# The first of a round's two C products issued ahead of the background products of the round before, and evictions of projections moved one round back

## The reference

```
q, k, v = split_heads(x @ W + b) for each of Wq, Wk, Wv      # (b, 16, 4096, 16)
scores   = q k^T / 4
sparsity = max(scores) - mean(scores)          # per query, over 4096 keys
top_idx  = the 307 queries of largest sparsity, per batch and head
out      = zeros; out[top_idx] = softmax(q[top_idx] k^T / 4) v
x = layernorm(x + out @ Wo + bo)
# then a mixing block with two gates:
xr, xk = mu * x + (1 - mu) * (x shifted by one token)
x = layernorm(x + sigmoid(xr @ W_r) * (relu(xk @ W_k)^2 @ W_v))
```

## Time and profile before

| what | value |
|---|---|
| time of 3 runs, median (lowest to highest) | 3449.08 us (3445.66 to 3450.98) |
| the profiled execution's own time | 3456.68 us |
| its span in the profile | 3454.9 us |
| PE, DVE, ACT, POOL busy over the span | 90%, 85%, 83%, 43% |
| granted clock of TensorE, mean over the span | 0.97 |

### The profile page before, as it was taken

How to read it: one execution, slowest core, us unless ns; L and a number is a source line. 1 busy time by engine, 2 the same in 40 slices (tenths; PEclk the granted TensorE clock), 3 DMA queues, 4 the chain that set the end, 5 groups by cost and what they waited for, 6 DMA issues and landing times.

```text
span 3454.9 us, 58997 instructions
## 1 busy us (share of the span) xinstructions
PE 3099.2 (90%) x15985; PEld 1433.1 (41%) x15985; DVE 2950.1 (85%) x5969; ACT 2873.2 (83%) x6445; POOL 1482.1 (43%) x2619
## 2 busy tenths in 40 slices
PE   6999999998899998998999888899988898897678
PEld 3334333343344433433444344444444443344466
DVE  4989988899979888888899888888988898886578
ACT  5889888889779999899899877699977699894555
POOL 2210022100136643553456356665555653447744
PEclk8999999999999999999999999999999999997899
DMA  6333222216021251141021251211142131013122
GB/s 178 80 100 113 64 75 82 82 30 18 15 44 32 39 33 31 33 33 32 19 36 31 46 48 42 49 37 35 31 41 48 35 33 32 14 20 15 19 79 69
DMA packets 262608, 163.63 MB, mean 47 GB/s; under 512 B 167877, under 2 KB 241797, under 8 KB 258181
## 3 DMA queue, kind: packets, MB, share of 16 engines
q1 hardware_dynamic: 254181, 156.41, 25.0%
q0 software_dynamic: 6144, 1.37, 0.5%
q10 hardware_dynamic: 1952, 2.10, 0.2%
HBM read 111.86 MB, written 47.86 MB: 46 GB/s over the span
## 4 chain that ended last, share of the span: by engine, by line
ACT 29%; PE 27%; issue 20%; DVE 19%; POOL 2%; DMA 1%; ACTq 0%; DVEq 0%; SPq 0%; POOLq 0%
ACT AB L941 21%; DVE JK L1100 11%; PE CP L669 8%; PE DP L673 7%; ACT E L979 5%; ACT msk L962 2%; PE PV L780 1%; PE PV L781 1%; PE BP L765 1%; PE BP L615 1%; DVE VF L1311 1%; DVE fst L1270 1%; DVE SPr L1100 1%; PE PV L803 1%; PE PV L615 1%
## 5 line engine op out<-in xcount | busy, mean ns | idle before, releaser
L1100 DVE CUSTOM_DVE_ANT_0 JK<-DP,AB 128x1024 bf16<-128x1024 f32 x2048 | 2468.0, 1222 | 366.5 <-DVE SPr L1100 129.9
L941 ACT ACTIVATE AB<-CP 128x512 f32<-128x512 f32 x4096 | 2226.6, 598 | 282.7 <-PE CP L669 234.2
L669 PE MATMUL CP<-KS,QS 128*128 128x512 f16 x4096 | 1424.0, 388 | 94.7 <-ACT AB L941 20.1
L673 PE MATMUL DP<-KS,QS 128*128 128x512 f16 x4096 | 1236.9, 384 | 61.1 <-DVE SPr L1100 54.6
L1506 POOL TENSOR_TENSOR SCR<-E 128x307 f16<-128x307 f32 x953 | 661.8, 707 | 585.1 <-ACT E L979 578.3
L669 PEld LDWEIGHTS CP<-KS,QS 128*128 128x128 f16 x4096 | 392.3, 96 | 887.5 <-ACT AB L941 752.7
L673 PEld LDWEIGHTS DP<-KS,QS 128*128 128x128 f16 x4096 | 360.9, 98 | 386.0 <-DVE SPr L1100 171.0
L979 ACT ACTIVATE E<-BP 128x307 f32<-128x307 f32 x871 | 379.6, 436 | 30.3 <-PE BP L765 29.2
L1355 POOL TENSOR_SCALAR SCR<-SCR 128x48 f16<-128x48 f16 (+2 forms) x122 | 49.2, 403 | 540.6 <-DVE SCR L1066 316.4
L765 PE MATMUL BP<-QT,KA 128*128 128x307 f16 x871 | 258.3, 297 | 20.4 <-ACT QT L971 18.4
L780 PE MATMUL PV<-E,XT 128*128 128x307 bf16 x512 | 161.0, 315 | 26.6 <-POOL SCR L1506 25.9
(11 more groups left out here) (369 smaller groups left out, 2997.3 us busy)
## 6 DMA issues: line engine op xcount, KB each, us to landing
KS<-KTC SPq DMA_DIRECT2D x256, 128.0 KB
QS<-QSC SPq DMA_DIRECT2D x512, 64.0 KB
KA<-KTC SPq DMA_DIRECT2D x128, 128.0 KB
QN<-SCR SPq DMA_DIRECT2D x16, 544.0 KB, 3.5
SCR<-in_L_attn_x SPq DMA_DIRECT2D x16, 512.0 KB, 6.3
AO<-E SPq DMA_DIRECT2D x16, 512.0 KB, 7.1
VF<-in_L_attn_x SPq DMA_DIRECT2D x64, 128.0 KB, 2.2
VF<-AO SPq DMA_DIRECT2D x64, 128.0 KB, 2.2
```

What stands on the lines that cost most here:

```text
L669: pe.matmul(o, qs, ks[j][:, 1, :], start=True, stop=True).then_inc(sc_c, 1)
L673: r = pe.matmul(o[:, 512 * j:512 * j + 512], qs, ks[j][:, 0, :], start=True, stop=True)
L941: act.activation(AB[p % 3][:, 512 * j:512 * j + 512], BANK["C%d" % j], ACT.Abs).then_inc(ab_full, 1)
L1100: dve.tensor_tensor_reduce(out=JK[p % 2][:], in0=BANK["D%d" % u], in1=AB[p % 3][:], scale=1.0, scalar=-3.0e38, op0=ALU.add, op1=ALU.max, a ...
```

## The change

Two things are moved and nothing is added or removed.

First, the C0 product of round p + 1 becomes a token of its own, `lead`. Where the background or attention step of round p holds one of `pv`, `xt`, `kmm`, `qmm`, `qtr`, `val`, this token is put right ahead of the first such token. So for an attention step PE now runs C1, D, D, score product, C0 of the next round, value product, value product; and in a projection round C1, D, D, C0 of the next round, then the two products. 1231 of the 2047 rounds get such a lead. In the others C0 is issued at the start of its round as before.

Second, the evictions are tokens of their own (`xtev`, `kev`, `qev`, `qtev`, `vev`). While rounds run, they stand one step later, behind the part of `main` of the next round on ACT and DVE; only the key projections that DVE evicts (`hi` = 0) and everything in the start (`fast`) keep their place. A bank whose eviction is late is not given to the next product (`state["late"]`).

```diff
-            if b != state["open"]:
+            if b not in (state["open"], state["late"]):
                 return b
...
             for hi in (1, 0):
                 bk = state["open"] = bank()
+                evict = [("kev", b, half, c, hi, bk, fast)]
                 for part in range(3):
-                    yield [("kmm", b, half, c, hi, part, bk, fast)]
+                    step = waiting + [("kmm", b, half, c, hi, part, bk, fast)]
+                    waiting = []
+                    if part == 2:
+                        state["open"], state["late"] = None, bk if hi and not fast else None
+                    yield step + (evict if part == 2 and (fast or not hi) else [])
+                    if part == 2 and hi and not fast:
+                        waiting, state["late"] = evict, None
...
+    def with_lead(step, p):
+
+        for i, token in enumerate(step):
+            if token[0] in ("pv", "xt", "kmm", "qmm", "qtr", "val") and p + 1 < NB * H * NP:
+                return step[:i] + [("lead", p + 1)] + step[i:]
+        return step
...
-            plan.extend(step or [])
+            plan.extend(with_lead(step or [], n * NP + p))
...
+            def lead_(p):
+                n = p // NP
+                led.add(p)
                 if p % NP == 0:
-                    pe.wait_ge(l_k[i], 128 * (n // 2 + 1))
+                    pe.wait_ge(l_k[n % 2], 128 * (n // 2 + 1))
                 if p % 32 == 0:
                     pe.wait_ge(l_h[p // 32 % 2], 128 * (n + 1))
...
+                qs, ks = scores(p)
+                o = claim("C0")
+                pe.matmul(o, qs, ks[0][:, 1, :], start=True, stop=True).then_inc(sc_c, 1)
+                owed["C0"] = ((ab_full, 2 * p + 1),)
+
+            def main(p):
+                u = p % 2
+                if p not in led:
+                    lead_(p)
+                qs, ks = scores(p)
+                o = claim("C1")
+                pe.matmul(o, qs, ks[1][:, 1, :], start=True, stop=True).then_inc(sc_c, 1)
+                owed["C1"] = ((ab_full, 2 * p + 2),)
```

More of the change, by code:

```diff
@@ L113, in product @@
         def product(c):
+            waiting = []
             for j in range(2):
                 bk = state["open"] = bank()
+                evict = [("qev", b, half, c, j, bk, fast)]
                 for part in range(3):
-                    yield [("qmm", b, half, c, j, part, bk, fast)]
-                state["open"] = None
+                    step = waiting + [("qmm", b, half, c, j, part, bk, fast)]
+                    waiting = []
+                    if part == 2:
+                        state["open"], state["late"] = None, None if fast else bk
+                    yield step + (evict if part == 2 and fast else [])
+                state["late"] = None
+                waiting = [] if fast else evict
+            if not fast:
+                yield waiting + [("split", k0 + c, "q", b, half, c, fast)]
         def store(c):
+            waiting = []
             for j in range(2):
-                yield [("qtr", b, half, c, j, bank(), fast)]
-            yield [("qstore", b, half, c)]
+                bk = bank()
+                evict = [("qtev", b, half, c, j, bk)]
+                state["late"] = None if fast else bk
+                yield waiting + [("qtr", b, half, c, j, bk, fast)] + (evict if fast else [])
+                waiting, state["late"] = [] if fast else evict, None
+            yield waiting + [("qstore", b, half, c)]
         if fast:
@@ L145, in values @@
                     bk = state["open"] = bank()
-                yield [("val", b, t, part, bk)] + ([("azero", t // 16, t // 2 % 8)] if b == 0 and t % 2 + part == 0 else [])
-            state["open"] = None
+                step = waiting + [("val", b, t, part, bk)]
+                waiting = []
+                if part == 2:
+                    state["open"], state["late"] = None, bk
+                yield step + ([("azero", t // 16, t // 2 % 8)] if b == 0 and t % 2 + part == 0 else [])
+            waiting, state["late"] = [("vev", b, t, bk)], None
+        yield waiting
     def select(g):
@@ L879, in xt, with kev @@
                                accum_out=xpart[:, k, c:c + 1]).then_inc(xt_act, 1)
-            def kmm(b, half, c, hi, part, bank, fast):
-                if part == 2 and hi:
+            def kev(b, half, c, hi, bank, fast):
+                if hi:
                     m = (2 * b + half) * 4 + c
@@ L1057, in kbar, with kev @@
                 dve.tensor_tensor(cols[:, SH], cols[:, BK], cols[:, KB], ALU.subtract).then_inc(kb_dve, 1)
-            def kmm(b, half, c, hi, part, bank, fast):
-                if part == 2 and not hi:
+            def kev(b, half, c, hi, bank, fast):
+                if not hi:
                     m = (2 * b + half) * 4 + c
```

62 lines of the change are left out of this document (30 added, 32 removed).

## The result

The changed kernel takes 3397.91 us (median of 4 runs, 3396.41 to 3403.29) against 3447.76 us for the kernel before (4 runs). The ratio is 0.9857, with a 95% interval of 0.9845 to 0.9869. That is 50 us less, 1.4%; I had forecast 3390.

The account below looks back on a forecast made before the run. No engine saturates throughout; a PE-ACT wait loop, closed by PE's order, was taken to set attention and projection rounds. Gains of 23 + 1 + 3 + 4 + 12 + 9 + 4 + 3 = 59 us from 3449 gave 3390, range 3350 to 3430.

Parts of the forecast that it names:

- Attention, 23 us: 622 plain attention rounds fall from 1.337 us to ACT's floor of 1.300, gaining 0.037 each, 23 us.
- The loop: Attention: PE and ACT wait for each other, 2.66 us per two rounds; C0 ahead of value products makes it 2.39.
- The moved wait: Attention: PE stands 0.05 to 0.08 us at C0, replacing the old wait at C1, so it costs nothing.
- The sign that I had given: Attention stretch: rounds of 1.30, ACT without gaps, a short wait of C0's load and nearly none for C1.
- the bubble stays: Rival, chance 0.12: the wait only moves from C1 to C0, attention gains nothing, projections half; 3426 us.
- slower: Rival, chance 0.08: C0's exposed weight load and semaphore add to PE's attention rounds, 1.40 us each; 3484 us.
- More: Rival, chance 0.17: evictions are hidden and ACT goes a bit under 1.30 in attention; 94 us gained, 3355 us.
- It does nothing: Rival, chance 0.05: ACT's and DVE's total work bounds the kernel at the same length; 3449 us.
- First rounds of a head, value products alone: 16 first rounds gain about 0.16 us each, 3 us; 30 value-product rounds go from 1.27 to 1.144, 4 us.
- Query chunks with their transposes, 9 + 4 us: Six product rounds 8.42 us against 9.03, 14 chunks, 9 us; transposes 4.2 against 4.47, 14 times, 4 us.
- Key chunks, 12 us: Key projections: six rounds take 8.14 us against 9.17, with eviction stalls of 0.28 and 0.12; 12 chunks, 12 us.
- Value projections, 3 us: Value projection rounds go from 1.275 us to 1.257, set by DVE's floor; 192 rounds, 3 us.

Follow-up runs that it names:

- second profile: The kernel before, unedited, profiled once more: 3449.28 us, where the execution profiled first took 3456.68.
- the swap: Changed kernel with the two halves of a key chunk in the other order, the half DVE evicts first: 3393.16 us, ratio 0.9853 to the kernel before.
- the experiment on the bank: Changed kernel, but a value projection isn't given the bank whose eviction stands in its own step: 3389.55 us, ratio 0.9838 to the kernel before.

## Why the prediction was right

The time lies in the range and the gain is 50 us where I had 59. The mechanism of the largest term, attention, is shown. That the total came so near is in part luck: all terms of the forecast lie in the 2048 rounds, and there the change gains 43 us, not 59. The start and the tail, on which the forecast had put nothing, gave another 8 between the two first profiles. By the steps:

- **Attention, 23 us.** Summed over the 622 rounds the changed kernel takes 811.6 us; the kernel before took 838.0, and 836.7 in its second profile. That is 25 us. The loop, PE's order as its cause and ACT as the next bound are each shown: by the product left out in the kernel before (1.297), by the same in the changed one (no change), and by the shorter exponential (1.261). A round of the stretch is 1.296, not 1.300; the mean of all 622 is 1.305, from 1.347. The 45 rounds with one-hot work, for which I had 1 us, lose 1.5 instead (75.2 to 76.7); no experiment looks into that.
- **The moved wait.** I had put 0.05 to 0.08 us of standing on PE at C0; its products show 0.02. The sign that I had given, a short wait of the load for C0 and nearly none for C1, came out only in part: the loads wait 0.26 and 0.16, and the one for C1 still stands 0.05 us behind the end of ACT's pair (it was 0.04). Both fit in a round that ACT sets. So the rivals "the bubble stays" and "slower" are refuted, with attention rounds at 1.296. "More" is refuted too: attention stopped at ACT's bound, and the evictions were not hidden. "It does nothing" is refuted by the time.
- **First rounds of a head, value products alone.** 3 and 4 us forecast; 2.7 (16 rounds, 41.6 to 38.9 us) and 3.7 (30 rounds, 38.1 to 34.4).
- **Query chunks with their transposes, 9 + 4 us.** Measured 0.85 a chunk, 12 us for 14. The six product rounds take 8.02, which is 7.74 and the one stall of 0.28; the second eviction lands in the round behind them. The stalls of 0.28 and 0.40 for an eviction on ACT were 0.26 (rounds of 1.55 against 1.29) and 0.41 (1.55 against 1.144).
- **Key chunks, 12 us.** Mis-sized. Six rounds take 8.54, not 8.14, and the chunk gains 0.63, 7 us for 12. The stall for DVE's eviction was taken as 0.12 and is 0.52: the third round takes 1.81. The prediction gives no working for its 0.12. Behind this eviction come rounds in which DVE itself is the bound, so none of its time is won back there. Placed first, in front of rounds that PE bounds, it costs 0.22, which the swap shows.
- **Value projections, 3 us.** Where they run by themselves the gain is there: 96 rounds from 122.37 to 120.33. Beside the search the change costs 10 us, which the prediction missed. It had taken 3 us for all 192 rounds from DVE's floor and had put no term on which bank the next projection draws. The bank drawn too early accounts for these 10, as the rounds with a value projection show (57.1 to 47.1 us in the experiment on the bank). The stretch also holds 29 rounds with a value projection where it held 27: the late evictions add one round behind the first batch's value projections and one behind the transposes of the input, so later background work stands two rounds later.
- **The start and the tail** were 4 us each shorter in the changed kernel's profile than in that of before. The start was between 60.2 and 67.0 us long in the traces of this study, whatever the edit, so I put nothing on it. The tail took 336.3 and 335.9 us in the two profiles of the kernel before and 331.6 to 334.5 in the kernels that move C0 or the evictions and leave all products in; why is open.

Against the second profile of the kernel before, the rounds sum up to 3044.7 - 3001.3 = 43 us: 25 (attention) + 7 (key) + 12 (query) + 3 (first rounds of a head) + 4 (value products alone) + 2 (value projections by themselves) = 53 gained, 10 given back in the search stretch.

That the two moves help in projections only together was nowhere in the prediction. I had costed the lead and the late eviction as one.

## What to carry to other kernels

When two engines hand single buffers to and fro, walk the loop over two turns and sum it from starts in the timeline. What one engine does between two products that the other waits for is in the loop even if that engine is not the bound, and moving it out of the loop pays until some engine's own work is the bound. A product that is issued earlier needs the consumer's queue in the same order: an early C0 whose reader stands behind an eviction that waits for a later product made query chunks longer than no change at all (18.25 against 16.95 us). And when the release of a buffer is moved later, look at who else draws from that pool, in the stretch where most draw from it. A cost that is read from one kind of stretch, here value projections without the search, need not hold where two kinds of work meet.

## What the runs showed of the hardware

ACT's instructions read as longer when ACT is the bound. In the changed kernel the absolute value's mean is 621 ns against 598 for the same 4096 instructions, and the exponential's 476 against 436, though the rounds are shorter. By stretch it is plainer. The rows are the absolute value in the attention stretch of the kernel before, in its five rounds without value products (where ACT was the bound already), in the attention stretch of the changed kernel, and there with the shorter exponential, where PE is the bound:

```profile
L941 ACT ACTIVATE AB<-CP 128x512 f32<-128x512 f32 x53 | 28.8, 596 | 0.2
L941 ACT ACTIVATE AB<-CP 128x512 f32<-128x512 f32 x10 | 5.8, 676 | 0.0
L993 ACT ACTIVATE AB<-CP 128x512 f32<-128x512 f32 x53 | 30.6, 670 | 0.0
L993 ACT ACTIVATE AB<-CP 128x512 f32<-128x512 f32 x53 | 28.8, 600 | 0.1
```

A mean of 670 to 676 ns goes with ACT as the bound, one of 596 to 600 with another bound. In the kernel before with one value product left out, at 1.297 us a round, it is 643. The busy share doesn't tell the two apart: ACT reads 34.60 of 34.75 us busy in the attention stretch of the kernel before, where the same work then took 33.69.

PE's busy time says as little: 33.66 of 33.69 us with three products of 307 columns a round, 33.55 of 33.69 with two.
